# Mamba scan states in SBUF instead of PSUM, decays two steps ahead, four product buffers, mean square on GpSimd

## The chip, the cores and the metric

The kernel runs on one core of a Trainium2 chip. The time is the device time of one launch in microseconds, the median of several runs. The engines are TensorE (PE, with its weight loads as PEld), VectorE (DVE), ScalarE (ACT), GpSimd (POOL) and SyncE (SP), which issues most of the DMAs. They run their own instruction streams and meet only through semaphores.

## The reference

Input `x` is 2 x 2048 tokens of 256 numbers, all in fp32. There are three layers:

```python
x = x + 0.5 * ffn(layernorm(x))     # 8 experts, top 2, capacity 640 a choice
x = x + attn(layernorm(x))          # the Mamba block and a small MLP
x = x + 0.5 * ffn(layernorm(x))
```

The change is in the middle one, where

```python
def attn(x):
    x = x + mamba(rmsnorm(x))
    h = square(relu(rmsnorm(x) @ c_fc_w.T))
    return x + h @ c_proj_w.T

# in mamba: x_conv, z, dt, B and C are projections; 512 channels, 16 states
A = -exp(A_log)
def step(h, inp):
    dt_t, B_t, C_t, u_t = inp
    dA = exp(dt_t[..., None] * A)
    h = h * dA + (dt_t * u_t)[..., None] * B_t[:, None, :]
    y = einsum('bes,bs->be', h, C_t)
    return (h, y)
y = (ys + x_conv * D) * silu(z)
return y @ out_proj_w.T
```

## The kernel before, in words

The program has five parts in a row: routing, experts, `mamba` (the middle layer), routing, experts. Only `mamba` is touched.

`mamba` works in 8 chunks ("turns", index `k`) of 512 tokens. Channels lie on the 128 partitions, in 4 groups `e`, and a turn takes the groups in 2 pairs `p`. For each pair it goes through the 16 states `s`: 32 steps a turn, numbered `n = 16 p + s`, 256 steps in all. One step does, for the two groups of the pair (index `j`):

- ACT: the decay `exp(dt * A)` into a PSUM bank (function `decay`; line 1084 is the helper that records every ACT instruction).
- POOL: `dB = DTU * B` for both groups in one instruction of 1024 elements (line 1260), from the product `DTU` and a row `B` that SP has broadcast into `BC`.
- DVE: the scan over the 512 tokens (line 1363) for each group, `h = h * decay + dB`; a product with `C`, "weigh", for each group into `G` (line 1372); between these two, a copy of the last column of both states into `ST`, masked to zero where a batch ends (line 1379).
- PE: adds each `G` into the output's PSUM bank with an identity matrix (line 1076), two matmuls a step.

The PSUM has 8 banks. Banks 0 and 1 serve all projections in turn, 2 and 3 hold the decays (`B_DA`), 4 and 5 the scan's states (`B_H`), 6 and 7 the output (`B_Y`). So there is one step's worth of decays, and ACT computes those of step `n + 1` after the scans of step `n`. `dB` and `G` have two buffers each.

After a pair's 16 steps `gated` (line 1332) multiplies the two output banks by `silu(z)` into `T3`; before it, line 1327 waits for all of the pair's products on PE. For pair 0 this stands at step 16 behind the scans, for pair 1 at step 0 of the next turn.

The rest of a chunk's work is spread over the steps of the turns around it, by three tables that give for each item the step at which PE, ACT, DVE and POOL do it. `EARLY` is the front of the next chunk: norm, transposes, input projection (`x`, `z`), convolution (`c`, four matmuls with diagonal matrices each, PE items 9, 10, 13 and 14), silu (ACT item 19, with a load of the activation table before and after it), `dt` and its softplus. `LATE` is what is left of it, in the chunk's own turn. `BACK` is the rest of the previous chunk: output projection, RMS norm, MLP. On POOL the items are `add` and `du` (lines 1235 and 1239, 1024 elements each, at steps 27, 28, 6 and 7), `xa` (line 1249, 512 elements, at steps 12 and 14) and the power -1/2 for the RMS norm (line 1245, step 10). On DVE they are `out`, `pj` and `v` (line 1344), which turns ACT's sum of squares `ssq`, 4 numbers a partition, into mean plus eps, at step 8.

An engine does its step's main work first and then the items of that step, DVE its scans first; PE does its items before the step's two products.

## Time and profile before

| | |
|---|---|
| median of 3 runs | 2199.52 us (2195.18 to 2201.32) |
| the profiled execution, its own time | 2204.47 us |
| its span, first to last instruction | 2202.7 us |
| mean granted TensorE clock | 0.941 of full speed |
| busy share of the span | PE 84%, DVE 78%, POOL 56%, ACT 44% |
| first dB product of the stage | 593.4 us |
| last scan of the stage | 1628.1 us |

A share is of the whole span, an average over five parts with different limits. What the change can move lies between the last two rows of the table. Matmul times are modelled in part, and consecutive DVE instructions overlap in the records by some 0.08 us: the next is issued while the last one drains. So the distance from start to start is what a busy DVE pays for an instruction, and the duration is a little more.

### The profile page before, as it was taken

Reading aid. Unit: us, or ns where it says so; the run is one execution under the profiler, and the core shown is the slowest. Engines: PE = TensorE matmul, PEld = TensorE weight load, DVE = VectorE, ACT = ScalarE, POOL = GpSimd, SP = SyncE. Lnnn points to the kernel's source line nnn. Section 1 sums busy time; section 2 is a strip of 40 time slices with the busy share of each in tenths; the row PEclk is TensorE's granted clock in tenths of the full one; section 3 lists DMA queues with packets and bytes.
Section 4 is the critical chain, followed back from the end, with each engine's and each line's share of the span. In section 5 each row is a group of like instructions: output and inputs, shape, how many; then the busy total and the mean of one; then the engine's idle time right before and its main releaser. Section 6 shows DMA issues by size and latency. Waiting matters only on the chain. (4 is left out here: it accounts for less than half of the span.)

```text
span 2202.7 us, 32882 instructions
## 1 busy us (share of the span) xinstructions
PE 1847.9 (84%) x9384; PEld 1306.7 (59%) x9385; DVE 1709.4 (78%) x2990; ACT 968.6 (44%) x1475; POOL 1241.5 (56%) x751
## 2 busy tenths in 40 slices
PE   6379998993887899989999898998577469999996
PEld 6269998993332435434344444434245369999996
DVE  4757667665498989989898999989965667667665
ACT  1333333331455556566655557655441333332331
POOL 1246555555465757667576676757631236555555
PEclk9999999997899999999999999999996579999998
DMA  6244343333333434434343434334412334343442
GB/s 197 72 112 100 80 84 82 81 70 100 115 129 124 134 124 135 133 129 132 125 136 118 133 124 135 134 125 134 143 53 77 115 97 97 80 86 82 85 75 27
DMA packets 160991, 237.52 MB, mean 108 GB/s; under 512 B 29370, under 2 KB 85296, under 8 KB 160304
## 3 DMA queue, kind: packets, MB, share of 16 engines
q1 hardware_dynamic: 130096, 198.84, 28.4%
q0 software_dynamic: 30720, 36.53, 10.0%
q8 instruction: 88, 1.44, 0.3%
q14 instruction: 87, 0.71, 0.1%
HBM read 202.57 MB, written 38.34 MB: 109 GB/s over the span
## 5 line engine op out<-in xcount | busy, mean ns | idle before, releaser
L1260 POOL TENSOR_TENSOR m_dB<-m_DTU,m_BC 128x1024 f32<-128x1024 f32 x256 | 602.8, 2358 | 328.3 <-DVE PS L1363 327.7
L1363 DVE TENSOR_TENSOR_SCAN PS<-PS,m_ST,m_dB 128x512 f32<-128x512 f32 x512 | 629.5, 1276 | 58.3 <-POOL m_dB L1260 27.1
L1076 PE MATMUL PS<-m_G,keep_ident 128*128 128x512 f32 x1024 | 499.4, 612 | 81.6 <-DVE m_G L1372 81.5
L1084 ACT ACTIVATE PS<-m_DT,m_A 128x512 f32<-128x512 f32 x512 | 353.4, 693 | 393.2 <-DVE PS L1363 390.8
L1076 PEld LDWEIGHTS PS<-m_G,keep_ident 128*128 128x128 f32 x1024 | 186.2, 191 | 342.4 <-DVE m_G L1372 211.7
L1372 DVE TENSOR_TENSOR m_G<-PS,m_BC 128x512 f32<-128x512 f32 x512 | 342.1, 679 | 2.9 <-PE PS L1076 2.9
L603 PE MATMUL PS<-e_xh,e_wh 128*128 128x256 f32 x1008 | 293.5, 291 | 0.3 <-DVEq L491 0.2
L603 PE MATMUL PS<-e_xl,e_wh 128*128 128x256 f32 x1008 | 287.4, 285 | 0.0
L603 PE MATMUL PS<-e_xh,e_wl 128*128 128x256 f32 x1008 | 286.9, 285 | 0.0
L621 PE MATMUL PS<-e_wh,e_hh 128*128 128x256 f32 x1008 | 281.6, 279 | 0.0
L660 ACT ACTIVATE e_hh<-e_u 128x512 fp32r<-128x512 f32 x252 | 158.3, 635 | 278.4 <-DVE e_u L716 262.3
L621 PE MATMUL PS<-e_wl,e_hh 128*128 128x256 f32 x1008 | 280.7, 278 | 0.0
L621 PE MATMUL PS<-e_wh,e_hl 128*128 128x256 f32 x1008 | 280.2, 278 | 0.0
L528 POOL DMA_INDIRECT e_xin<-xrows,e_gix x160 | 199.6, 1248 | 57.5 <-issue 45.6
L534 POOL DMA_INDIRECT out<-e_ysb,e_six x80 | 134.5, 1681 | 153.5 <-DVE e_ysb L740 136.5
L534 POOL DMA_INDIRECT sums<-e_ysb,e_six x80 | 135.6, 1696 | 151.3 <-DVE e_ysb L740 134.1
L735 DVE TENSOR_TENSOR e_ysb<-PS,e_b 128x512 f32<-128x512 f32 x80 | 55.2, 691 | 188.7 <-PE PS L621 185.0
L603 PEld LDWEIGHTS PS<-e_xh,e_wh 128*128 128x128 f32 x1008 | 197.1, 196 | 1.0 <-DVEq L491 0.6
L603 PEld LDWEIGHTS PS<-e_xl,e_wh 128*128 128x128 f32 x1008 | 197.1, 196 | 0.0
L603 PEld LDWEIGHTS PS<-e_xh,e_wl 128*128 128x128 f32 x1008 | 195.8, 194 | 0.0
L716 DVE TENSOR_TENSOR e_u<-PS,keep_b 128x512 f32<-128x512 f32 x252 | 170.1, 688 | 25.6 <-PE PS L603 14.1
L621 PEld LDWEIGHTS PS<-e_wl,e_hh 128*128 128x128 f32 x1008 | 189.3, 188 | 0.0
(195 smaller groups left out, 2797.0 us busy)
## 6 DMA issues: line engine op xcount, KB each, us to landing
m_BC<-bc_rows SPq DMA_DIRECT2D x512, 256.0 KB, 3.3
layer_raw<-w SPq DMA_DIRECT2D x64, 512.0 KB
xrows<-r_xn SPq DMA_DIRECT2D x16, 512.0 KB, 4.3
keep_X<-x SPq DMA_DIRECT2D x4, 1024.0 KB, 9.4
sums<-keep_X SPq DMA_DIRECT2D x4, 1024.0 KB, 11.2
out<-keep_X SPq DMA_DIRECT2D x4, 1024.0 KB, 11.1
keep_X<-sums SPq DMA_DIRECT2D x3, 1024.0 KB, 13.3
e_xin<-xrows,e_gix POOLq DMA_INDIRECT x160
```

Of the source, the lines that this page charges most:

```text
L528: G.indirect_dma_start(out=xin[:, c % CPE, t, :], out_offset=None, in_=xrows, in_offset=column(gix, c, t), bounds_check=last_token, oob_is ...
L534: G.indirect_dma_start(out=sums, out_offset=column(six, c, t), in_=ysb[:, c % CPE, t, :], in_offset=None, compute_op=ALU.add, bounds_check ...
L603: last = M(PS[:, B_S1 + pair, m * CH:(m + 1) * CH], a, r, start=(n == 0), stop=(n == len(terms) - 1))
L621: last = M(PS[:, B_Y + c % 2, t * D:(t + 1) * D], a, r, start=(n == 0), stop=(n == len(terms) - 1))
L660: A(hh[:, c % 2, 2 * pair:2 * pair + 2, :], u[:, pair, :, :], ACT.Relu).then_inc(hh_ok, 1)
L716: V.tensor_tensor(u[:, pair, :, :], PS[:, B_S1 + pair, :].rearrange("p (m c) -> p m c", m=2), b1.unsqueeze(2).to_broadcast([P, 2, CH]), AL ...
L735: V.tensor_tensor(ysb[:, c % CPE, :, :], PS[:, B_Y + c % 2, :].rearrange("p (t d) -> p t d", t=CHT), b2.unsqueeze(1).to_broadcast([P, CHT, ...
L1076: last = M(PS[:, B_Y + j, :], C["ident"][:, :], G[:, s % 2, j, :], start=False, stop=(s == DS - 1))
L1084: return nc.scalar.activation(out, in_, func, **kw)
L1260: G_.tensor_tensor(dB[:, s % 2, :, :], DTU[:, es, :], BC[:, s % NBC, 0:1, :].to_broadcast([P, 2, CT]), ALU.mult).then_inc(dB_ok, 1)
L1363: V.tensor_tensor_scan(PS[:, B_H + j, :], PS[:, B_DA + j, :], dB[:, s % 2, j, :], ST[:, s, e:e + 1], ALU.mult, ALU.add).then_inc(scanned, 1)
L1372: V.tensor_tensor(G[:, s % 2, j, :], PS[:, B_H + j, :], BC[:, s % NBC, 1, :], ALU.mult).then_inc(g_ok, 1)
```

## The change

- The scan's output goes to a new SBUF buffer `HS` (two of a pair's size) instead of PSUM banks 4 and 5. The weighing product and the state copy read it there.
- The freed banks hold decays: four banks, two steps' worth. ACT computes the decays of step `n + 2` after the scans of step `n` (`AHEAD = 2`).
- `G` gets four buffers (`NG`) instead of two.
- `v` leaves DVE. ACT's squares are scaled by 1/16 before squaring, so the sum is already the mean; POOL adds eps from a small tile and takes the power, at step 9.
- `T3` and `HID` share one tile `TH` of six groups instead of two tiles of four; the gate product of pair 1 also waits for the last MLP projection of the chunk before.

```diff
+        eps = sb("eps", [P, CTT])
-        T3 = sb("T3", [P, EK, CT])
-        HID = sb("HID", [P, EK, CT])
+        TH = sb("TH", [P, 6, CT])
+        T3 = TH[:, 0:EK, :]
+        def hid(e, n=1):
+            at = e + 4 if e < 2 else e
+            return TH[:, at:at + n, :]
-        G = sb("G", [P, 2, 2, CT])
+        NG, NH = 4, 2
+        G = sb("G", [P, NG, 2, CT])
+        HS = sb("HS", [P, NH, 2, CT])
-        B_DA, B_H, B_Y = 2, 4, 6
+        B_DA, B_Y, AHEAD = 2, 6, 2
-            ..., ("v", 0): (_, _, 8, 10),
+            ..., ("v", 0): (_, _, _, 9),
...
# ACT
-                        last = F(XR[:, t, :], XP[:, t, :], ACT.Square, accum_out=ssq[:, t:t + 1])
+                        last = F(XR[:, t, :], XP[:, t, :], ACT.Square, scale=1.0 / math.isqrt(D), accum_out=ssq[:, t:t + 1])
-                    if not (is_first(k) and n == 0):
-                        act.wait_ge(scanned, k * (2 * STEPS) + (2 * (n - 1) + j + 1))
-                    F(PS[:, B_DA + j, :], DT[:, e, :], ACT.Exp, scale=A[:, e, s:s + 1]).then_inc(dA_ok, 1)
+                    if not (is_first(k) and n < AHEAD):
+                        act.wait_ge(scanned, k * (2 * STEPS) + (2 * (n - AHEAD) + j + 1))
+                    F(PS[:, B_DA + 2 * (n % AHEAD) + j, :], DT[:, e, :], ACT.Exp, scale=A[:, e, s:s + 1]).then_inc(dA_ok, 1)
...
# POOL
                 if kind == "v":
+                    gp.wait_ge(sq_ok, k + 1)
+                    G_.tensor_tensor(ssq[:, :], ssq[:, :], eps[:, :], ALU.add).then_inc(v_ok, 1)
                     gp.wait_ge(v_ok, k + 1)
                     G_.tensor_tensor(ssq[:, :], ssq[:, :], mhalf[:, 0, 0:CTT], ALU.pow).then_inc(rs_ok, 1)
...
# DVE
+                if p == 1 and not (is_first(k)):
+                    wait_written(dve, ("pj", 1), k - 1)
                 V.tensor_tensor(T3[:, es, :], PS[:, B_Y:B_Y + 2, :], SZ[:, par, es, :], ALU.mult).then_inc(yz_ok, 1)
-                elif kind == "v":
-                    dve.wait_ge(sq_ok, k + 1)
-                    V.tensor_scalar(ssq[:, :], ssq[:, :], 1.0 / D, RMS_EPS, ALU.mult, ALU.add).then_inc(v_ok, 1)
-                            if not (is_first(k) and n == 0):
-                                dve.wait_ge(g_ok, k * (2 * STEPS) + (2 * n + j - 1))
-                                dve.wait_ge(kept, k * STEPS + n)
+                            if not (is_first(k) and n < NH):
+                                dve.wait_ge(g_ok, k * (2 * STEPS) + (2 * (n - NH) + j + 1))
+                                dve.wait_ge(kept, k * STEPS + (n - NH + 1))
-                            V.tensor_tensor_scan(PS[:, B_H + j, :], PS[:, B_DA + j, :], dB[:, s % 2, j, :], ST[:, s, e:e + 1],
+                            V.tensor_tensor_scan(HS[:, n % NH, j, :], PS[:, B_DA + 2 * (n % AHEAD) + j, :], dB[:, s % 2, j, :], ST[:, s, e:e + 1],
                                                  ALU.mult, ALU.add).then_inc(scanned, 1)
-                            V.tensor_tensor(G[:, s % 2, j, :], PS[:, B_H + j, :], BC[:, s % NBC, 1, :], ALU.mult).then_inc(g_ok, 1)
+                            V.tensor_tensor(G[:, n % NG, j, :], HS[:, n % NH, j, :], BC[:, s % NBC, 1, :], ALU.mult).then_inc(g_ok, 1)
-                        if not (is_first(k) and n < 2):
-                            dve.wait_ge(g_read, k * STEPS + (n - 1))
+                        if not (is_first(k) and n < NG):
+                            dve.wait_ge(g_read, k * STEPS + (n - NG + 1))
-                        V.tensor_tensor(ST[:, s, 2 * p:2 * p + 2].bitcast(U32), PS[:, B_H:B_H + 2, CT - 1].bitcast(U32),
+                        V.tensor_tensor(ST[:, s, 2 * p:2 * p + 2].bitcast(U32), HS[:, n % NH, :, CT - 1].bitcast(U32),
                                         mask[:, bass.ds(k + 1, 1)].to_broadcast([P, 2]), ALU.bitwise_and).then_inc(kept, 1)
```

## Rows read from the trace of the kernel before

**Rows 1.** Stretches of 128 us from 721 to 1489 us: sum and mean

```profile
sum 768.00, PE 710.38 PEld 329.96 DVE 718.04 ACT 470.77 POOL 515.33; mean PE 118.40 PEld 54.99 DVE 119.67 ACT 78.46 POOL 85.89
```

**Rows 2.** Timeline, one step: start us, us, engine line op

```profile
906.79 2.45 DVE L1363 TENSOR_TENSOR_SCAN PS<-PS,m_ST,m_dB 128x512 f32<-128x512 f32 x2
...
909.15 0.67 DVE L1372 TENSOR_TENSOR m_G<-PS,m_BC 128x512 f32<-128x512 f32 x1
...
909.32 2.35 POOL L1260 TENSOR_TENSOR m_dB<-m_DTU,m_BC 128x1024 f32<-128x1024 f32 x1
...
910.40 2.45 DVE L1363 TENSOR_TENSOR_SCAN PS<-PS,m_ST,m_dB 128x512 f32<-128x512 f32 x2
```

**Rows 3.** Waits of DVE in the stage: us in total, times, longest

```profile
DVE PS L1363 <- ACT PS L1084: 26.6, 8, 3.7
DVE m_T L1332 <- issue: 20.8, 6, 3.5
```

**Rows 4.** Timeline of DVE, two idle times: [idle before <-releaser]

```profile
794.49 1.22 DVE L1332 TENSOR_TENSOR m_T<-PS,m_SZ 128x1024 f32<-128x1024 f32 x1 [3.47 <-issue]
...
815.04 2.47 DVE L1363 TENSOR_TENSOR_SCAN PS<-PS,m_ST,m_dB 128x512 f32<-128x512 f32 x2 [3.47 <-ACT PS L1084]
```

**Rows 5.** Timeline of DVE, routing: sixteen scans of 32 elements

```profile
73.43 2.10 DVE L261 TENSOR_TENSOR_SCAN r_inc<-r_zcol,r_tot 128x32 f32<-128x32 f32 x16
```

**Rows 6.** Groups by line and form, DVE and POOL: busy, mean ns | idle

```profile
L1363 DVE TENSOR_TENSOR_SCAN PS<-PS,m_ST,m_dB 128x512 f32<-128x512 f32 x512 | 629.5, 1276 | 58.3 <-POOL m_dB L1260 27.1 <-ACT PS L1084 26.6 <-issue 3.8
L1372 DVE TENSOR_TENSOR m_G<-PS,m_BC 128x512 f32<-128x512 f32 x512 | 342.1, 679 | 2.9 <-PE PS L1076 2.9
...
L1332 DVE TENSOR_TENSOR m_T<-PS,m_SZ 128x1024 f32<-128x1024 f32 x16 | 19.5, 1216 | 27.3 <-issue 20.8 <-PE PS L1076 6.5
...
L261 DVE TENSOR_TENSOR_SCAN r_inc<-r_zcol,r_tot 128x32 f32<-128x32 f32 x32 | 4.2, 209 | 0.1
...
L264 DVE SCALAR_TENSOR_TENSOR r_pos<-r_pos,r_tot 128x512 f32<-128x512 f32 x2 | 1.4, 692 | 0.1
...
L1260 POOL TENSOR_TENSOR m_dB<-m_DTU,m_BC 128x1024 f32<-128x1024 f32 x256 | 602.8, 2358 | 328.3 <-DVE PS L1363 327.7
...
L1235 POOL TENSOR_TENSOR m_DT<-m_DT,m_sp 128x1024 f32<-128x1024 f32 x16 | 37.7, 2356 | 21.4 <-ACT m_sp L1084 21.4
...
L1249 POOL TENSOR_TENSOR keep_X<-keep_X,m_XP 128x512 f32 x12 | 15.2, 1269 | 0.0
```

**Rows 7.** Timeline of DVE and POOL, expert stage, 404 to 410 us

```profile
404.98 1.28 POOL L516 COPY e_gix<-layer_token 128x10 uint32 x1
...
405.55 0.68 DVE L721 SCALAR_TENSOR_TENSOR e_hl<-e_u,e_hh 128x512 fp32r<-128x512 f32 x1
...
409.76 0.20 POOL L516 COPY e_six<-layer_dest 128x10 uint32 x1
```

**Rows 8.** Line 1344: duration ns, min/median/max, first and last start

```profile
L1344 DVE TENSOR_SCALAR m_ssq<-m_ssq x8: 170/1308/1368, 762.0 to 1645.0; 128x4 f32<-128x4 f32 x8
```

**Rows 9.** Timeline around one of them, POOL and DVE

```profile
760.95 2.36 POOL L1260 TENSOR_TENSOR m_dB<-m_DTU,m_BC 128x1024 f32<-128x1024 f32 x1 [0.65 <-DVE PS L1363]
...
762.03 1.31 DVE L1344 TENSOR_SCALAR m_ssq<-m_ssq 128x4 f32<-128x4 f32 x1
```

**Rows 10.** Timelines of DVE and POOL, routing stage, 83 to 97 us

```profile
83.41 5.46 POOL L341 TENSOR_TENSOR r_hot<-r_count,r_high 128x320 f32<-128x320 f32 x8 [45.76 <-DVEq L288]
...
83.44 5.48 DVE L298 TENSOR_SCALAR r_inlow<-r_count_b,r_low 128x128 bf16<-128x128 bf16 x8 [0.46 <-DVE r_high L287]
...
90.95 0.88 DVE L302 TENSOR_TENSOR r_inblock<-r_hot,r_tile_no 128x320 bf16<-128x320 f32 x2
...
91.22 1.19 POOL L341 TENSOR_TENSOR r_hot<-r_count,r_high 128x320 f32<-128x320 f32 x1 [2.34 <-PE PS L409]
...
91.75 1.39 DVE L298 TENSOR_SCALAR r_inlow<-r_count_b,r_low 128x128 bf16<-128x128 bf16 x2
...
95.81 1.38 DVE L298 TENSOR_SCALAR r_inlow<-r_count_b,r_low 128x128 bf16<-128x128 bf16 x8
```

More of the change, by code:

```diff
@@ L1 @@
+import math
 import concourse.bass as bass
@@ L845, in mamba @@
         BACK = {
-            ("out", 0): (1, _, 2, _), ("out", 1): (3, _, 4, _), ("sq", 0): (_, 7, _, _), ("v", 0): (_, _, 8, 10),
+            ("out", 0): (1, _, 2, _), ("out", 1): (3, _, 4, _), ("sq", 0): (_, 7, _, _), ("v", 0): (_, _, _, 9),
             ("hr", 0): (_, 11, _, _), ("hT", 0): (19, 20, _, _), ("hT", 1): (21, 22, _, _), ("xa", 0): (_, _, _, 12), ("xa", 1): (_, _, _, 14),
@@ L1043, in back @@
                 if kind in ("out", "pj"):
-                    at, ready, src = (W_OUT, yz_ok, T3) if kind == "out" else (W_PJ, q_ok, HID)
+                    at, ready, src = (W_OUT, yz_ok, lambda e: T3[:, e:e + 1, :]) if kind == "out" else (W_PJ, q_ok, hid)
                     pe.wait_ge(ready, k * 2 + 2)
@@ L1048, in back @@
                         for e in range(EK):
-                            last = M(bank(p, k)[:, (t % 2) * D:(t % 2 + 1) * D], src[:, e, t * P:(t + 1) * P],
+                            last = M(bank(p, k)[:, (t % 2) * D:(t % 2 + 1) * D], src(e)[:, 0, t * P:(t + 1) * P],
                                      weights(at, D, e, 0, D), start=(e == 0), stop=(e == EK - 1))
@@ L1075, in turn @@
                             pe.wait_ge(g_ok, k * (2 * STEPS) + (2 * n + j + 1))
-                            last = M(PS[:, B_Y + j, :], C["ident"][:, :], G[:, s % 2, j, :], start=False, stop=(s == DS - 1))
+                            last = M(PS[:, B_Y + j, :], C["ident"][:, :], G[:, n % NG, j, :], start=False, stop=(s == DS - 1))
                         last.then_inc(g_read, 1)
@@ L1177, in back @@
                     wait_written(act, p, k)
-                    F(HID[:, n, :], bank(p, k), ACT.Relu).then_inc(read(p, k), 1)
+                    F(hid(n)[:, 0, :], bank(p, k), ACT.Relu).then_inc(read(p, k), 1)
                 elif kind == "q":
                     wait_read(act, k, ("fc", 2 * n), ("fc", 2 * n + 1))
-                    F(HID[:, 2 * n:2 * n + 2, :], HID[:, 2 * n:2 * n + 2, :], ACT.Square).then_inc(q_ok, 1)
+                    F(hid(2 * n, 2), hid(2 * n, 2), ACT.Square).then_inc(q_ok, 1)
             def decay(k, p, s):
@@ L1191, in decay @@
                     e, n = 2 * p + j, p * DS + s
-                    if not (is_first(k) and n == 0):
-                        act.wait_ge(scanned, k * (2 * STEPS) + (2 * (n - 1) + j + 1))
-                    F(PS[:, B_DA + j, :], DT[:, e, :], ACT.Exp, scale=A[:, e, s:s + 1]).then_inc(dA_ok, 1)
+                    if not (is_first(k) and n < AHEAD):
+                        act.wait_ge(scanned, k * (2 * STEPS) + (2 * (n - AHEAD) + j + 1))
+                    F(PS[:, B_DA + 2 * (n % AHEAD) + j, :], DT[:, e, :], ACT.Exp, scale=A[:, e, s:s + 1]).then_inc(dA_ok, 1)
             def turn(k, par, has_front, has_back):
                 if is_first(k):
-                    decay(k, 0, 0)
+                    for s in range(AHEAD):
+                        decay(k, 0, s)
                 for p in range(PAIRS):
@@ L1201, in turn @@
                         n = p * DS + s
[L1202 to L1203 removed]
+                        if n + AHEAD < STEPS:
+                            decay(k, (n + AHEAD) // DS, (n + AHEAD) % DS)
                         elif has_front:
[L1205 removed]
+                            decay(k + 1, 0, n + AHEAD - STEPS)
                         if is_first(k) and n == FIRST_SILU_AT:
@@ L1270, in _ @@
             V.memset(mhalf[:, :, :], -0.5)
+            V.memset(eps[:, :], RMS_EPS)
             V.memset(fmask[:, :], 1.0)
```

3 lines of the change are left out of this document (removed).

## The prediction

> **What bounds the kernel now.** I read the page first: TensorE (PE) and VectorE (DVE) are the busy engines, and the state-space stage, between the two expert stages, is the only part that the change touches. The view by stretches, cut in pieces of 128 us, about a chunk of 512 tokens each, gives a mean of 119.7 us busy for DVE, 118.4 for PE, 85.9 for GpSimd (POOL) and 78.5 for ScalarE (ACT) [rows 1]. So DVE sets the pace and PE is right behind.
>
> The timeline of one step shows what the DVE time is made of [rows 2]. Two scans are issued at 906.79 and the first product at 909.15, so a scan takes 1.18 us from issue to issue; the product, the small state copy and the second product take 1.25 us (909.15 to 910.40). A step is 3.61 us, without a gap. POOL's dB product, 2.36 us, starts at 909.32, just after the scans end, because it waits for the buffer that they read. It runs beside the two weighing products and is over before the next pair of scans is.
>
> The waits of DVE [rows 3] have two sources that come in every turn: a scan that waits for ACT (26.6 us in 8 waits), and the gate product of line 1332, which waits for PE (20.8 us in 6 waits put down to "issue"; line 1327 asks for every product of the pair). One of each is seen at its place [rows 4]: 3.47 us at 794.49, 3.47 us at 815.04.
>
> **What each part changes.**
>
> *States to SBUF, scan side.* A scan of 32 elements from SBUF to SBUF is issued every 131 ns (16 in 2.10 us) [rows 5]; the one of 512 every 1180 [rows 2]. How much of that is the element and how much a fixed part, neither row tells alone. Products of 512 and 1024 elements take 679 and 1216 ns, 1.05 ns an element; a scan's element needs about twice that, for the two scans, 209 and 1276 ns, lie 2.2 ns an element apart [rows 6]. At exactly twice, 2.10 ns, the 480 further elements cost 1008 ns, and a scan of 512 into SBUF would be issued every 1139 ns, 41 less than now; the recorded durations, treated the same way, give 209 + 1008 = 1217 against 1276, 59 less. Either would be the price of writing PSUM. At 2.19 ns an element there is no such price, and no row shows a slower write to SBUF: bounds 0 and 60 ns. I take 45, near the value from the issue times, which are what a busy engine pays: 512 x 0.045 = 23 us, bounds 0 and 31. In seven of a turn's 32 steps it is lost again, because PE sets the pace between its convolution items (9 to 14) and the gate wait at step 16: 18 us remain.
>
> *States to SBUF, product side.* The product now reads HS and BC, both in SBUF; so does the state copy (HS and the mask). A product of PSUM with SBUF takes 679 ns, a two-input one of the same size with both in SBUF 692 [rows 6]: nothing gained by itself, at most 0.02 us lost. The Trainium skill ("VectorE: DVE Perf Modes", the errata section) has a fixed cost of 58 cycles from SBUF and 120 from PSUM, which would save 65 ns on each of 512 products, 33 us, and put the forecast at 2180. The two rows of this kernel show no such saving, and I use the rows.
>
> *Two SBUF inputs beside POOL.* This is the cost that the diff doesn't name. In the expert stage POOL copies 10 numbers in 0.20 us when DVE is elsewhere, but one that starts at 404.98 takes 1.28 and ends at 406.26, and a DVE instruction with two SBUF inputs (e_u, e_hh) runs from 405.55 to 406.23 [rows 7]: the copy ends 0.03 us after it. The other way round, the 4-element tensor_scalar of line 1344 takes 170 ns once and 1308 in the median [rows 8]; at 762.03 it lasts 1.31 and ends at 763.34, where the dB product begun at 760.95 ends at 763.31 [rows 9]. In the routing stage eight tensor_scalars take 5.48 us beside eight POOL products of 5.46, and 1.38 us without them [rows 10]. So the two engines exclude each other for the length of the reading. The Trainium skill ("SBUF — State Buffer", "Who interferes with whom") says it as a rule: an instruction of VectorE with two SBUF inputs and one of GpSimd that reads SBUF take the same read port in turn, the later blocks fully. The rows agree with it.
>
> By these rows the 512 products and 256 copies, 1.25 us a step, will exclude POOL's 2.36 us, which they now overlap.
>
> What that costs depends on who gets in when. A POOL product waiting behind two DVE products issued back to back (90.95, 0.88 for two) took 1.19 us, to 92.41, where eight unhindered take 0.68 each [rows 10]: counted back from its end it began about when the next DVE instruction was issued (91.75), so its delay covers both and it did not slip in between. If this holds, dB(n+2) waits until the second product is done and runs during the next scans. From a first product at time 0: product, copy, product to 1.25; dB then needs its 2.36, less the tail after its last read (0.14: line 1344 without a wait would have begun at 763.34 - 0.17 = 763.17, and dB ended at 763.31) and less a start-up of a few hundredths that it has behind it, so the port is free at about 3.45. The next product is due at 1.25 + 2 x 1.135 = 3.52 (3.61 if the scan gains nothing). It just fits: no cost a step, and up to 0.1 if a handover is slower, 26 us over 256 steps.
>
> There is no room left in a step, so every other POOL product delays DVE. Those of lines 1235 and 1239, 30 within the stage, have dB's shape and its 2.36 us [rows 6]; their reading holds the port 2.2: 30 x 2.2 = 66 us. Bounds: 33, if half of them fall beside DVE's one-input work, and 66. Those of line 1249 (1.27 us, 14 within the stage, 1.12 each, 15.7 us) stand at items 12 and 14, in front of the gate wait of 3.47 where DVE waits for PE anyhow: nothing, bound 15.7.
>
> *Decays two steps ahead.* ACT does a turn's silu, with a table load before and after it, and the decays stand behind that. With one more step done the scan has 3.5 us more in hand, and the wait was 3.47: the 26.6 us go. Bounds 20 and 26.6.
>
> *Four product buffers.* DVE hardly waits for them; the gate wait is PE's own backlog, which more buffers don't work off. Nothing.
>
> *Mean square on POOL.* Line 1344 goes from DVE: 7 x 1.2 = 8.4 us gained (a wait of 1.31 less the 0.1 that a short instruction takes from issue to issue [rows 9]). POOL gets a 4-element add of some 0.2 us between dB products, and now waits itself for ACT's squares, with its next dB product queued behind; dB is needed a step and a half later, so that hides. T3 and HID sharing a tile adds a wait of the gate product for PE's last projection, which was issued two steps before it and is included in the wait for all products: nothing.
>
> **Sum.** 66 - 18 - 26.6 - 8.4 = +13 us. The sum is made in the profiled execution, 2204.5 us, so 2217.5 there; it stands 5 us above the median of the runs, 2199.5, from which the forecast is 2212.5. Bounds of this case: 33 - 31 x 25/32 - 26.6 - 8.4 = -26 (2173); and 66 + 26 + 15.7 - 0 - 20 - 8.4 = +79 (2279).
>
> **The rivals.**
> *POOL slips in between the products.* If POOL's waiting dB gets the port when the first product is done, the copy and the second product wait out 2.2 us in each of 256 steps: 563 us, with the rest 2199.5 + 563 + 13 = 2,775. For it: eight tensor_scalars and eight POOL products take turns, so a DVE instruction does not keep the port for the next of its kind [rows 10]. Against it: the pair of two-input products at 90.95; but of the 0.27 us from 90.95 to POOL's start only some 0.17 were left to the first one's end, and here POOL will have waited about 0.5.
> *No exclusion that matters* (the other side, faster). If two-input products go beside POOL's reading, or POOL's reading leaves gaps, what remains is -18 - 26.6 - 8.4 = -53, 2146. It decides where POOL's 30 extra products cost under 1.5 us each in place of 2.2 (30 x 1.5 = 45, sum under -6.6). For it: no row shows a two-input tensor_tensor of DVE held up by POOL, only tensor_scalars. Against it: the copy that waits in [rows 7]. PE would allow it: 118.4 busy in 128 us becomes 97% of a turn 5% shorter.
> *The port is shared, but the scan gains nothing*: +31, 2230. *The products gain 65 ns each by leaving PSUM*: 13 - 33, 2180; [rows 6] speak against it, 0.02. Both lie in the first case's range and are counted with it.
>
> **How the numbers follow.** Port in turn, with DVE keeping it through a step: 0.60. POOL slips in: 0.20. No exclusion that matters: 0.20. The first gives 2212.5; its own range is 2173 to 2279, a fifth of it below 2193, a fifth within 0.3% of the median (6.6 us, about what a measurement of this kernel can tell), three fifths above 2206. So faster 0.12 + 0.20 = 0.32, same 0.12, slower 0.36 + 0.20 = 0.56. The range takes in the first and third case, with 8 us below 2146 for the upper bound of the scan's gain, 2138 to 2280, and leaves out the second.
>
> **What the profile of the changed kernel would show.** The scan near 1230 ns in place of 1276. The step from scan to scan at about 3.5 us in quiet stretches, dB products that start just behind the scans but last about 3.5 us in place of 2.36, products of 0.69 us that a few times a turn last near 2.9, next to lines 1235, 1239 and 1249. The wait for ACT near 815 gone, the gate wait still there but shorter. It is wrong if the state copy or second product lasts over 2 us in every step (POOL slips in), if dB stays at 2.36 beside products of 0.69 (no exclusion), or if the scan keeps 1276.

## The result: 21% slower, and all of it in one wait per step

| | before | after |
|---|---|---|
| median of 4 runs, us | 2199.64 (2195.18 to 2201.32) | 2661.97 (2660.71 to 2663.10) |
| ratio, 95% interval | 1 | 1.2106, 1.2085 to 1.2126 |
| the profiled execution: time, span | 2204.47, 2202.7 | 2660.71, 2658.6 |
| stage: start of the first scan to start of the last | 595.9 to 1628.1: 1032.2 | 591.8 to 2084.4: 1492.7 |
| a full turn, first scan to first scan | 129 to 131 | 187.8 (the first 185.2) |

The stage is 460 us longer; the medians differ by 462, the profiled spans by 456. What stands ahead of the stage and behind it took what it took before, within 5 us.

**The groups of the stage**, by line and form (DVE, then POOL), which answer to [rows 6]. L1394 is the state copy, L1387 the product, L1378 the scan, L1274 the dB product:

```profile
L1378 DVE TENSOR_TENSOR_SCAN m_HS<-PS,m_ST,m_dB 128x512 f32<-128x512 f32 x512 | 626.0, 1261 | 25.9 <-POOL m_dB L1274 25.9
L1394 DVE TENSOR_TENSOR m_ST<-m_HS,m_mask 128x2 uint32<-128x2 uint32 x256 | 552.6, 2159 | 0.0
L1387 DVE TENSOR_TENSOR m_G<-m_HS,m_BC 128x512 f32<-128x512 f32 x512 | 361.5, 706 | 0.0
...
L1350 DVE TENSOR_TENSOR m_TH<-PS,m_SZ 128x1024 f32<-128x1024 f32 x16 | 19.1, 1194 | 1.1 <-issue 1.1
```

```profile
L1274 POOL TENSOR_TENSOR m_dB<-m_DTU,m_BC 128x1024 f32<-128x1024 f32 x256 | 683.4, 2670 | 684.2 <-DVE m_HS L1378 684.1
L1251 POOL TENSOR_TENSOR m_DTU<-m_DT,m_U 128x1024 f32<-128x1024 f32 x16 | 45.3, 2833 | 0.1
L1247 POOL TENSOR_TENSOR m_DT<-m_DT,m_sp 128x1024 f32<-128x1024 f32 x16 | 43.8, 2739 | 15.7 <-ACT m_sp L1095 14.7
```

The copy moves two numbers a partition and takes 2159 ns in the mean. The same copy of before stood in this row:

```profile
L1379 DVE TENSOR_TENSOR m_ST<-PS,m_mask 128x2 uint32<-128x2 uint32 x256 | 38.0, 148 | 0.0
```

**One step on the timeline**, DVE and then POOL, which answers to [rows 2]:

```profile
1208.45 0.66 DVE L1387 TENSOR_TENSOR m_G<-m_HS,m_BC 128x512 f32<-128x512 f32 x1
1209.03 2.30 DVE L1394 TENSOR_TENSOR m_ST<-m_HS,m_mask 128x2 uint32<-128x2 uint32 x1
1211.26 0.68 DVE L1387 TENSOR_TENSOR m_G<-m_HS,m_BC 128x512 f32<-128x512 f32 x1
1211.86 2.44 DVE L1378 TENSOR_TENSOR_SCAN m_HS<-PS,m_ST,m_dB 128x512 f32<-128x512 f32 x2
1214.23 0.66 DVE L1387 TENSOR_TENSOR m_G<-m_HS,m_BC 128x512 f32<-128x512 f32 x1
```

```profile
1208.61 2.71 POOL L1274 TENSOR_TENSOR m_dB<-m_DTU,m_BC 128x1024 f32<-128x1024 f32 x1 [3.07 <-DVE m_HS L1378]
```

Read the two together. DVE's first product starts at 1208.45 and ends at 1209.11. dB starts at 1208.61 and lasts 2.71 where it lasted 2.36, which is what it would last if its reading waited for that product's end. The copy is issued at 1209.03 and ends at 1211.33, when dB ends (1211.32). Then the second product runs undisturbed. The step is 5.78 us from product to product, against 3.61. Both engines read two SBUF operands, and here they take turns instruction by instruction. That is the rival "POOL slips in between the products", to which the prediction gave 0.20.

The trap in this view is that no wait shows. DVE has no idle time ahead of the copy; the wait is inside its duration, and DVE's busy share even rises (78% to 84%). An instruction of known size with a duration far over its own is the sign.

**The ledger of the stage**, in us: copies 552.6 - 38.0 = +515; products 361.5 - 342.1 = +19; waits ahead of the scans, 58.3 down to 25.9, -32; gate product, wait 27.3 down to 1.1, -26; line 1344 gone, -9; scans -3.5. Sum +463, measured +460. Busy time is the union of the instructions, so overlaps count once. The two first terms are 239 copies of over 2 us (the other 17 took 0.15) and 15 products of 1.93 to 2.01. Those 15 are the first product of every 16th step, where the gate product stands between the scans and the products: there dB has started 0.9 to 1.0 us ahead, so that the product waits and not the copy. PE was granted 0.84 of its clock from 600 to 2087 us and its products on line 1087 took 753 ns; DVE never waited for them but for the 1.1.

### The profile page after: what moved, and what is told of

The parts are those of the page before. It is cut to its first block and busy times, and to the rows that moved or that the text cites. A ratio compares the mean times of both kernels' runs of the same rounds, so it can differ in the third digit from the quotient of the medians.

```text
span 2658.6 us, 32902 instructions
## 1 busy us (share of the span) xinstructions
PE 2077.9 (78%) x9384; PEld 1332.2 (50%) x9385; DVE 2233.3 (84%) x2983; ACT 968.0 (36%) x1475; POOL 1349.6 (51%) x759
## 5 line engine op out<-in xcount | busy, mean ns | idle before, releaser
L1274 POOL TENSOR_TENSOR m_dB<-m_DTU,m_BC 128x1024 f32<-128x1024 f32 x256 | 683.4, 2670 | 684.2 <-DVE m_HS L1378 684.1
L1087 PE MATMUL PS<-m_G,keep_ident 128*128 128x512 f32 x1024 | 673.0, 753 | 336.1 <-DVE m_G L1387 330.8
L1378 DVE TENSOR_TENSOR_SCAN m_HS<-PS,m_ST,m_dB 128x512 f32<-128x512 f32 x512 | 626.0, 1261 | 25.9 <-POOL m_dB L1274 25.9
L1394 DVE TENSOR_TENSOR m_ST<-m_HS,m_mask 128x2 uint32<-128x2 uint32 x256 | 552.6, 2159 | 0.0
L1387 DVE TENSOR_TENSOR m_G<-m_HS,m_BC 128x512 f32<-128x512 f32 x512 | 361.5, 706 | 0.0
```

The lines of the kernel that those rows point to most:

```text
L1087: last = M(PS[:, B_Y + j, :], C["ident"][:, :], G[:, n % NG, j, :], start=False, stop=(s == DS - 1))
L1274: G_.tensor_tensor(dB[:, s % 2, :, :], DTU[:, es, :], BC[:, s % NBC, 0:1, :].to_broadcast([P, 2, CT]), ALU.mult).then_inc(dB_ok, 1)
L1378: V.tensor_tensor_scan(HS[:, n % NH, j, :], PS[:, B_DA + 2 * (n % AHEAD) + j, :], dB[:, s % 2, j, :], ST[:, s, e:e + 1], ALU.mult, ALU.add ...
L1387: V.tensor_tensor(G[:, n % NG, j, :], HS[:, n % NH, j, :], BC[:, s % NBC, 1, :], ALU.mult).then_inc(g_ok, 1)
L1394: V.tensor_tensor(ST[:, s, 2 * p:2 * p + 2].bitcast(U32), HS[:, n % NH, :, CT - 1].bitcast(U32), mask[:, bass.ds(k + 1, 1)].to_broadcast([ ...
```

## The experiments

Runs of one group shared a chip and the runs of the kernel before. A ratio is to before, with its 95% interval. A kernel without one ran once, and its last column gives the one time of before beside it, in us.

| run | us | ratio, or before beside it |
|---|---|---|
| dB waits for the products | 2261.1 | 1.0275 (1.0249 to 1.0301) |
| state copy on ScalarE | 2645.1 | 1.2017 (1.1986 to 1.2048) |
| PSUM states, the small parts only | 2198.5 | 0.9991 (0.9976 to 1.0006) |
| one SBUF input | 2194.5 | 0.9971 (0.9949 to 0.9993) |
| scans in place | 2219.9 | 1.0083 (1.0062 to 1.0104) |
| in place, decays early | 2182.5 | 0.9909 (0.9875 to 0.9942) |
| the same, z ahead of c | 2169.4 | 0.9855 (0.9823 to 0.9887) |
| z ahead of c, small parts only | 2181.2 | 0.9912 (0.9879 to 0.9944) |
| first product 208, 320 columns | 2582.3, 2611.9 | 2206.3 |
| no wait between, one signal | 2740.0, 2739.3 | 2199.6 |
| equal pair, wait in routing | 2645.2, 2196.2 | 2200.7 |
| bf16 products, third routing product | 2644.7, 2209.3 | 2193.0 |
| repeated factor, plain ones between | 2644.1, 2224.6 | 2204.2 |

### Is it the port, and when POOL asks for it?

**dB waits for the products.** One line of after, on POOL:

```diff
-                            gp.wait_ge(scanned, k * (2 * STEPS) + (2 * n - 2))
+                            gp.wait_ge(g_ok, k * (2 * STEPS) + (2 * n - 2))
```

> The changed kernel, with one wait altered: POOL's dB product waits for the two weighing products of the step (g_ok), not for its scans. If the whole loss comes from the read port being handed to a waiting dB product in front of the state copy, the copy is back at 0.15 us, the second product at 0.69, dB at 2.36 beside the scans, and the step falls from 5.78 to about 3.65 us (1.25 + 2.39); POOL's other large products then have no free port time of their own and cost up to 2.2 us each: 2190 to 2260, 2225 in the middle. If the copy is slow for a reason of its own (a read behind the scan's write to SBUF), it stays at 2.2 to 2.3 us and the kernel near 2660.

Measured: 2261.1, so 401 of the 462 us come back by moving one start. Timeline of DVE and of POOL, a crowded step and the start of a quiet one at 908.24:

```profile
906.18 1.47 DVE L1387 TENSOR_TENSOR m_G<-m_HS,m_BC 128x512 f32<-128x512 f32 x1
907.57 0.15 DVE L1394 TENSOR_TENSOR m_ST<-m_HS,m_mask 128x2 uint32<-128x2 uint32 x1
907.64 0.68 DVE L1387 TENSOR_TENSOR m_G<-m_HS,m_BC 128x512 f32<-128x512 f32 x1
908.24 2.45 DVE L1378 TENSOR_TENSOR_SCAN m_HS<-PS,m_ST,m_dB 128x512 f32<-128x512 f32 x2
```

```profile
904.74 2.35 POOL L1274 TENSOR_TENSOR m_dB<-m_DTU,m_BC 128x1024 f32<-128x1024 f32 x1
908.40 2.35 POOL L1274 TENSOR_TENSOR m_dB<-m_DTU,m_BC 128x1024 f32<-128x1024 f32 x1 [1.30 <-DVE m_G L1387]
```

dB now runs beside the scans, one of whose inputs is PSUM, and has its 2.35 back; the copy is 0.15 again. The product at 906.18 waits because that dB came late, behind the two POOL instructions of the mean square (902.6 to 904.8). This kernel is the schedule that the prediction described as its likeliest case, made by a semaphore, so it prices that case's terms. Of its 255 steps 162 are under 3.8 us: 117 take 3.62 to 3.66 and 45 take 3.71 to 3.74, where a quiet step of before takes 3.62. So the handover costs 0.04 in most steps and 0.10 in some, 0.05 in the mean and about 8 us in all. The extra POOL work: 37 copies over 0.3 us carry 64.5 us above 0.15 each, 15 products over 0.83 carry 17.6 above 0.68. By what POOL runs beside them, lines 1247 and 1251 cost 29.4 + 32.2 = 61.6 us (the prediction has 66), line 1263 15.0 (0, bound 15.7), and the mean square 7 x 0.79 = 5.5, which the prediction took to hide.

**The state copy on ScalarE.** After, with DVE's copy between the products taken out:

```diff
# ACT, after step n's decays
+                        act.wait_ge(scanned, k * (2 * STEPS) + (2 * n + 2))
+                        F(ST[:, s, 2 * p:2 * p + 2], HS[:, n % NH, :, CT - 1], ACT.Copy, scale=now[:, 0:1]).then_inc(kept, 1)
```

> The changed kernel with the state copy made by ACT, so that the two weighing products stand back to back on DVE with dB waiting behind the first. Theory 1 (a waiting POOL product gets the port at the first change of instruction after it asked, whatever follows): the second product lasts about 2.8 us in every step, the step stays near 5.7 us, 2630 to 2660. Theory 2 (DVE keeps the port from one product to the next of its kind, and only the state copy gave it away): the second product lasts 0.68, dB lasts about 3.5 from its start, the step is 3.6, 2190 to 2240.

Measured: 2645.1. Two products now follow each other on DVE, and the second takes the blow: 0.66, then 2.83, under a dB of 2.71 (the first line holds both, 3.42 from start to end).

```profile
902.86 3.42 DVE L1395 TENSOR_TENSOR m_G<-m_HS,m_BC 128x512 f32<-128x512 f32 x2
906.21 2.45 DVE L1386 TENSOR_TENSOR_SCAN m_HS<-PS,m_ST,m_dB 128x512 f32<-128x512 f32 x2
```

So the copy was no special victim: whatever comes second waits, and like instructions do not keep the port between them here.

**A first product of 208 and of 320 columns**, which shortens the time between POOL's start and DVE's next instruction (it leaves out the rest of the first product).

```diff
-                            V.tensor_tensor(G[:, n % NG, j, :], HS[:, n % NH, j, :], BC[:, s % NBC, 1, :], ALU.mult).then_inc(g_ok, 1)
+                            V.tensor_tensor(G[:, n % NG, j, 0:(208 if j == 0 else CT)], HS[:, n % NH, j, 0:(208 if j == 0 else CT)], BC[:, s % NBC, 1, 0:(208 if j == 0 else CT)], ALU.mult).then_inc(g_ok, 1)
```

> The changed kernel with the first product cut to 208 of its 512 columns (the rest of that product is left out and stays zero), so that DVE issues the state copy about 0.28 us after it and dB, which starts 0.155 us after the first product, has waited about 0.13 us at that moment, as the POOL product of the routing stage in [rows 10] had. If a POOL instruction asks for the port some time after its recorded start, longer than 0.13 us, the copy goes through in 0.15 us and the second product, issued 0.07 us later, waits instead (2.8 us). If it asks at once, the copy waits 2.3 us. If DVE keeps the port where instructions follow close, neither waits: a step of 3.3 us and under 2150.

> The same with 320 columns (the other 192 left out): the copy is issued about 0.40 us after the first product, and dB has waited about 0.24 us. If POOL asks within 0.24 us, the copy waits 2.3 us in every step, as with 512 columns; if later, the copy goes through and the second product waits 2.8 us.

```profile
1205.11 0.34 DVE L1388 TENSOR_TENSOR m_G<-m_HS,m_BC 128x208 f32<-128x208 f32 x1
1205.38 2.30 DVE L1395 TENSOR_TENSOR m_ST<-m_HS,m_mask 128x2 uint32<-128x2 uint32 x1
```

```profile
1205.27 2.39 POOL L1274 TENSOR_TENSOR m_dB<-m_DTU,m_BC 128x1024 f32<-128x1024 f32 x1 [3.07 <-DVE m_HS L1379]
```

The copy is issued 0.11 us after dB's start and still waits 2.30; with 320 columns the gap is 0.23 and the wait the same. An engine that has been waiting a tenth of a microsecond is served first.

**One SBUF input.** After, with the products' factor and the copy's mask read from PSUM banks that hold constants, and the decays one step ahead again to free those banks (it leaves out C's change from step to step and the reset between batches):

```diff
-                            V.tensor_tensor(G[:, n % NG, j, :], HS[:, n % NH, j, :], BC[:, s % NBC, 1, :], ALU.mult).then_inc(g_ok, 1)
+                            V.tensor_tensor(G[:, n % NG, j, :], HS[:, n % NH, j, :], PS[:, B_C, :], ALU.mult).then_inc(g_ok, 1)
...
-                        V.tensor_tensor(ST[:, s, 2 * p:2 * p + 2].bitcast(U32), HS[:, n % NH, :, CT - 1].bitcast(U32),
-                                        mask[:, bass.ds(k + 1, 1)].to_broadcast([P, 2]), ALU.bitwise_and).then_inc(kept, 1)
+                        V.tensor_tensor(ST[:, s, 2 * p:2 * p + 2], HS[:, n % NH, :, CT - 1],
+                                        PS[:, B_C + 1, 0:2], ALU.mult).then_inc(kept, 1)
```

> The changed kernel with its states in SBUF as they are, but with no DVE instruction of two SBUF inputs: both products read their factor from a PSUM bank that holds one row of C all along (left out: the C of each step), and the state copy is multiplied by ones in PSUM (left out: the reset between the two batches). Two of the four decay banks are taken for that, so the decays are one step ahead, as before. If the read port is the whole loss, the copy is back at 0.15, the products at 0.68, dB at 2.36 from just behind the scans, the step at 3.6, and the time at 2190 to 2205. If SBUF states cost something by themselves (a scan that writes SBUF, a read behind it), the time stays above 2215; if the scan gained 45 ns each, it falls below 2185.

```profile
L1383 DVE TENSOR_TENSOR_SCAN m_HS<-PS,m_ST,m_dB 128x512 f32<-128x512 f32 x512 | 628.3, 1270 | 36.6 <-ACT PS L1095 28.5 <-issue 4.1 <-POOL m_dB L1274 3.2
L1392 DVE TENSOR_TENSOR m_G<-m_HS,PS 128x512 f32<-128x512 f32 x512 | 340.3, 674 | 0.0
L1399 DVE TENSOR_TENSOR m_ST<-m_HS,PS 128x2 f32<-128x2 f32 x256 | 38.8, 152 | 0.0
```

2194.5, with dB at 2359 ns beside the products. The second SBUF operand is the whole loss. The states in SBUF cost nothing and give nothing that these runs can tell: the scan takes 1270 ns, the product 674 with one PSUM input, and the ratio (0.9949 to 0.9993) overlaps that of the next kernel, whose states are in PSUM (0.9976 to 1.0006). The Trainium skill ("SBUF — State Buffer", "Who interferes with whom") says that an instruction of VectorE with at most one SBUF input, outside its 2-port modes, does not contend with GpSimd, and that one with two SBUF inputs contends with a GpSimd instruction that reads SBUF. This run and after agree with both halves.

### What the other parts are worth

**PSUM states, the small parts only**: before, with the mean square on POOL, four product buffers and the shared tile, and nothing else.

```diff
-        G = sb("G", [P, 2, 2, CT])
+        G = sb("G", [P, 4, 2, CT])
...
-            ..., ("v", 0): (_, _, 8, 10),
+            ..., ("v", 0): (_, _, _, 9),
```

> The kernel before with three parts of the change: mean square finished by POOL, four product buffers, T3 and HID in one tile. The states stay in PSUM, the decays one step ahead. By the sum only the first counts: 7 x 1.2 us, so 8 us faster than before, 2191; the buffers nothing. A rival gives the buffers part of the gate wait (20.8 us): down to 2175.

2198.5: no difference that shows. Timeline of DVE at the two idle times of [rows 4]:

```profile
795.54 1.22 DVE L1346 TENSOR_TENSOR m_TH<-PS,m_SZ 128x1024 f32<-128x1024 f32 x1 [4.68 <-issue]
...
816.08 2.47 DVE L1374 TENSOR_TENSOR_SCAN PS<-PS,m_ST,m_dB 128x512 f32<-128x512 f32 x2 [3.59 <-ACT PS L1092]
```

The 1.2 us that DVE saved on line 1344 came back as 1.2 us more in front of the gate product (3.47 to 4.68), where PE sets the time. The interval of the ratio, 5 us faster to 1 us slower, leaves the term of 8.4 us out.

**Scans in place**, to get the decays ahead without SBUF states: the kernel above, with each scan written over its own decays in PSUM.

```diff
# the scan's output and first input
-                            PS[:, B_H + j, :], PS[:, B_DA + j, :]
+                            PS[:, B_DA + 2 * (n % 2) + j, :], PS[:, B_DA + 2 * (n % 2) + j, :]
# ACT, ahead of the decays of step n
-                        act.wait_ge(scanned, k * (2 * STEPS) + (2 * (n - 1) + j + 1))
+                        act.wait_ge(g_ok, k * (2 * STEPS) + (2 * (n - 2) + 2))
+                        act.wait_ge(kept, k * STEPS + (n - 2 + 1))
```

> As the kernel e3_psum_states, and each scan writes its states over its own decays in PSUM, so that four banks give decays two steps ahead without any SBUF state: the decays of step n + 2 wait for the products of step n. If the port is all that made the change slow, the wait for ACT (26.6 us) goes too: 2199.6 - 8 - 26 = 2165, products at 0.68, copy at 0.15, dB at 2.36. If PE's backlog at the gate product takes up what is gained, 2180 to 2191. If a scan in place is slower, its record shows it above 1276 ns.

> As e4_inplace, but the decays of step n + 1 wait for the products of step n - 1 and are issued in ACT's step n, so ACT's items come earlier than in the kernel before and not later, as they did in e4_inplace (2220). If the later items made e4_inplace slow, the wait for ACT falls from 3.5 to about 1 us a turn, the gate wait stays near 4.7: 2199 - 8 x 2.5 = 2180. If a turn's length is set by PE alone, what the ACT wait loses comes back at the gate, and the time stays within 5 us of 2199.

The first form, which issues the decays of step n + 2 after step n, is slower (2219.9). They now wait for the products, and ACT's items of each step stand behind them. The wait for ACT falls from 27.0 to 13.7 us, but the gate wait grows to 5.55 a turn, and the scans' wait for dB from 28.5 to 51.3 in all, because POOL's two long items of a turn start late and run back to back with dB (752 to 764 us). The second issues the decays of n + 1 ahead of step n's items, as before; it waits only for products long done. 2182.5: the wait for ACT falls from 27.0 us (longest 3.7) to 17.4 (2.2), all idle time ahead of the scans from 60.0 to 43.4, and the gate wait stays at 4.7. The scan takes 1276 ns in place as well.

**z ahead of c**: the front's z projections move to PE's steps 13 to 16 and the last two convolutions behind them, to 17 and 18, out of the way of the pair's last product. Once on the kernel above, once on the one with the small parts only.

```diff
-            ..., ("c", 2): (13, 14, _, _),
-            ("c", 3): (14, 15, _, _), ("z", 0): (15, 16, _, _), ("z", 1): (16, 17, _, _), ("z", 2): (17, 18, _, _),
-            ("z", 3): (18, 19, _, _), ...
+            ..., ("z", 0): (13, 14, _, _),
+            ("z", 1): (14, 15, _, _), ("z", 2): (15, 16, _, _), ("z", 3): (16, 17, _, _), ("c", 2): (17, 18, _, _),
+            ("c", 3): (18, 19, _, _), ...
```

> As e7_inplace_early, with PE's z projections moved from steps 15 to 18 to steps 13 to 16, and two of the four convolutions from 13 and 14 to 17 and 18. A convolution item costs PE 3.4 us on top of 1.7 for the products, 1.5 more than a DVE step; that backlog is what the gate product at step 16 waits for. If so, the gate wait of 3.5 to 4.7 us falls to about 1.5 and the time to 2180 - 25 = 2155; if the backlog only moves to the silu behind the convolutions, the wait for ACT grows by as much and the time stays at 2180.

> As e3_psum_states (2198.5), with the same swap of z and convolution items and nothing else. If the gate wait is PE's backlog of four convolutions, it falls by 3 us in each of 8 turns: 2175. If silu, now behind the last convolution at step 18, comes later by what the backlog is, the wait for ACT at step 20 grows from 3.5 to 6 us: 2198.

Groups of DVE in the combined kernel:

```profile
L1372 DVE TENSOR_TENSOR_SCAN PS<-PS,m_ST,m_dB 128x512 f32<-128x512 f32 x512 | 629.9, 1277 | 59.9 <-ACT PS L1092 35.7 <-POOL m_dB L1271 24.2
...
L1347 DVE TENSOR_TENSOR m_TH<-PS,m_SZ 128x1024 f32<-128x1024 f32 x16 | 19.5, 1216 | 12.0 <-issue 9.0 <-PE PS L1084 3.1
```

The gate wait falls from 36 us to 12 here and 13 in the other; part of it comes back as a wait for ACT, 17.4 to 35.7 us here and 27.0 to 34.2 in the other. Combined, 2169.4, the best here: 1.5% under before, with the states still in PSUM.

### Why did the pair in [rows 10] stay together?

The prediction had read its schedule from that pair. Eight more runs vary the pair, from the kernel with the copy on ScalarE or from before.

**No wait between, and no signal either**: both scans are waited for ahead of the first product; in the second run one signal covers both products.

```diff
-                            dve.wait_ge(scanned, k * (2 * STEPS) + (2 * n + j + 1))
+                            if j == 0:
+                                dve.wait_ge(scanned, k * (2 * STEPS) + (2 * n + 2))
```

> As e2_copy_on_act (2645: two products back to back, the second waits 2.2 us for dB), but both scans are waited for ahead of the first product, so the second has no wait of its own, as the second of the pair at 90.95 in the routing stage [rows 10] had none. If a wait in front of an instruction is what opens the port for POOL, the second product lasts 0.68, the step is 3.6 and the kernel about 2230. If not, the step stays at 5.7 and the time at 2645.

> As e12_no_wait_between, and the first product signals no semaphore (the second counts for both), so the pair is joined as the pair of the routing stage was: no wait and no signal between. If the signal at its end is what opens the port, 2230; if neither, 2645, and the routing pair was let through for something in its own shape (three-dimensional operands, 320 elements, bf16 out) or in POOL's.

```profile
1205.96 3.44 DVE L1396 TENSOR_TENSOR m_G<-m_HS,m_BC 128x512 f32<-128x512 f32 x2
```

```profile
1205.90 2.35 POOL L1282 TENSOR_TENSOR m_dB<-m_DTU,m_BC 128x1024 f32<-128x1024 f32 x1 [4.19 <-DVE m_HS L1386]
```

For dB neither answers. With both engines released by the same scan, dB starts 0.05 us ahead of the first product, and that one now waits: the pair was not parted, it was preceded. The step is 5.95 us, the longest of all.

POOL's other instructions answer in the same traces. In the second run 30 of them start during a first product, and all get in ahead of the second one, though nothing stands between the two: 12 of `du` (1024 elements; the second product then lasts 2.82), 12 of `xa` (512 elements; 1.75) and 6 additions of 4 numbers, which are over 0.14 us after the second product's start. DVE and POOL at one `xa`, where the first line holds both products, 2.84 behind dB and 1.75 behind `xa`:

```profile
1046.74 4.51 DVE L1396 TENSOR_TENSOR m_G<-m_HS,m_BC 128x512 f32<-128x512 f32 x2
```

```profile
1048.99 1.72 POOL L1271 TENSOR_TENSOR keep_X<-keep_X,m_XP 128x512 f32 x1
```

**An equal pair.** As the run without wait and signal, but both products read the first group's states, so that the first needs only the first scan (it leaves out the second group's products).

```diff
-                                dve.wait_ge(scanned, k * (2 * STEPS) + (2 * n + 2))
+                                dve.wait_ge(scanned, k * (2 * STEPS) + (2 * n + 1))
-                            last = V.tensor_tensor(G[:, n % NG, j, :], HS[:, n % NH, j, :], BC[:, s % NBC, 1, :], ALU.mult)
+                            last = V.tensor_tensor(G[:, n % NG, j, :], HS[:, n % NH, 0, :], BC[:, s % NBC, 1, :], ALU.mult)
```

> The kernel after with the state copy on ScalarE, the two products without a wait or a signal between them (both signals come with the second), and both of them multiplying the states of the pair's first group, so that the first can start as early as ever, beside the second scan's end (it leaves out the products of the second group, so the output is not the reference's). GpSimd's dB then starts behind the first product, as in the kernel after, and finds a DVE instruction queued with nothing between. Theory 1, what parted the products before was the wait or the signal between them, and two products with nothing between keep the port, as the pair of the routing stage does: the second product 0.66 us, dB about 3.3, step near 3.7, some 2,200 to 2,230 us. Theory 2, GpSimd gets the port at any change of instruction: second product 2.83, dB 2.71, step 5.7, about 2,645 us. In both, the start of dB must be read first: if it starts ahead of the first product, as in the two runs before, the run does not answer.

```profile
1003.36 3.43 DVE L1396 TENSOR_TENSOR m_G<-m_HS,m_BC 128x512 f32<-128x512 f32 x2
```

```profile
1003.51 2.72 POOL L1282 TENSOR_TENSOR m_dB<-m_DTU,m_BC 128x1024 f32<-128x1024 f32 x1 [2.99 <-DVE m_HS L1386]
```

dB starts 0.15 us after the first product, and the second, with nothing between the two, lasts 2.85: parted, 2645.2 us.

**A wait in routing**, the other way round:

```diff
                     for c in range(TOPK):
+                        dve.wait_ge(abs_ok, i * (2 * NH) + (2 * g + 2))
```

> The kernel before, with one more wait, already met, ahead of each of the two products of line 302 in the routing stages; nothing else is changed. Theory 1, a wait between two DVE instructions is what lets GpSimd in: the second product of the pair beside GpSimd's waiting one (90.95 in the trace of before) grows from 0.48 to about 1.1 us, and GpSimd's shrinks from 1.19 to about 0.9. Theory 2, the wait is nothing: 0.48 and 1.19 as before. The time of the whole kernel stays within 0.3% in both.

Still 0.48 each and 1.19 to 1.20 for POOL, in all four places of the two routing stages. Wait and signal have no part in it.

**The type of the output, the form of the factor, the time.** Four edits: `G` and its identity in bf16; the factor four numbers of C, each repeated 128 times; in routing a third product between the two; in routing three products with two plain factors between them.

```diff
-        G = sb("G", [P, NG, 2, CT])
+        G = sb("G", [P, NG, 2, CT], BF16)
...
# the factor of the products, the other two operands viewed as 4 x 128
-                                            BC[:, s % NBC, 1, :]
+                                            BC[:, s % NBC, 1, 0:4].unsqueeze(2).to_broadcast([P, 4, CT // 4])
...
# routing, between the two products of line 302
+                            for r in range(3):
+                                V.tensor_tensor(spare[:, g, r, :, :], hot[:, g, 0, :, :], hot[:, g, 1, :, :], ALU.mult)
```

> The kernel after with the state copy on ScalarE, and the products and their identity matrix on TensorE in bf16, which is what the pair of the routing stage writes. Theory 1, a product that writes 16-bit values is over sooner or keeps the port: second product near 0.66, step under 4 us, about 2,200 us. Theory 2, the type of the output has no part in it: second product 2.83, dB 2.71, step 5.7, about 2,645 us, as with fp32.

> The kernel before, with a third product of the same kind between the two of line 302 in the routing stages, into a tile of its own that nobody reads. GpSimd's instruction starts some 0.27 us after the first of them, so it sees two changes of a two-input instruction in place of one. Theory 1, at its start GpSimd is just too late for the first change and gets in at the next: the first two last 0.48 us, the third about 1.0, and GpSimd 1.19. Theory 2, these products keep the port between them whatever the time: all three last 0.48 and GpSimd about 1.6, until the next tensor_scalar. The whole kernel is longer by 8 to 20 us, 40 products or so at 0.40.

> The kernel after with the state copy on ScalarE, and products whose second factor is a repeated value: four numbers of C, each read for 128 elements, in place of 512 of them (it leaves out the rest of C, so the output is not the reference's). The pair of the routing stage reads its second factor so. Theory 1, an input that repeats one value leaves no two-input reading, or keeps the port: second product near 0.66, dB either 2.36 (no exclusion) or 3.3 (it waits for the pair), step 3.7, about 2,200 us. Theory 2, the factor's form has no part in it: second product 2.83, dB 2.71, step 5.7, about 2,645 us.

> The kernel before, with three products between the two of line 302 in the routing stages, whose two factors are both plain rows of 320 numbers in SBUF, into a tile that nobody reads. Theory 1, the repeated second factor of line 302 is what keeps the port: GpSimd, which starts during the first, gets in at a change of the plain ones, one of them lasts about 1.0 us or more, and GpSimd's instruction about 1.0 to 1.2. Theory 2, it is something of GpSimd's own instruction or of the stage: all five products last 0.48, and GpSimd about 2.4, until the next tensor_scalar. The kernel is longer by some 40 us (120 products at 0.40 is 48, less where the stage has time to spare).

In the Mamba stage the second product lasted 2.82 and 2.83 us. In routing three products stayed together; timeline of DVE and of POOL in the run with the third one:

```profile
97.94 0.48 DVE L303 TENSOR_TENSOR r_inblock<-r_hot,r_tile_no 128x320 bf16<-128x320 f32 x1
98.34 0.48 DVE L306 TENSOR_TENSOR r_spare<-r_hot,r_tile_no 128x320 bf16<-128x320 f32 x1
98.74 0.48 DVE L303 TENSOR_TENSOR r_inblock<-r_hot,r_tile_no 128x320 bf16<-128x320 f32 x1
99.14 1.38 DVE L299 TENSOR_SCALAR r_inlow<-r_count_b,r_low 128x128 bf16<-128x128 bf16 x2
```

```profile
98.19 1.60 POOL L345 TENSOR_TENSOR r_hot<-r_count,r_high 128x320 f32<-128x320 f32 x1 [3.06 <-PE PS L413]
```

POOL waits through two changes of instruction, ends 0.05 us ahead of the first tensor_scalar (99.14, 0.70) and so got the port at the change to it. With three plain products between the two, all five lasted 0.48 and POOL 2.40. Both runs show it in all four places. So the reading of [rows 10] was right: there DVE keeps the port through two, three and five such products. It did not carry over to the Mamba stage. Excluded as the reason, each taken by itself, are a wait, a signal, the output's type, a repeated factor, and being just too late; so is the length of POOL's instruction, as those of 1024, 512 and 4 elements all got in. What remains are the length of the products (320 against 512, though a 320-column product followed by the copy was parted), and the form of POOL's instruction, which in routing subtracts two operands that are both repeated. No run tells these apart, or tests two features at once; the cause stays open.

## Why the prediction was wrong

**The step that failed** is the one in "What that costs depends on who gets in when": that a waiting dB "did not slip in between" and would run behind the second product. In place of it, POOL was served at DVE's first change of instruction, in 239 of 256 steps, at 2.15 us each, and the range of 2138 to 2280 had left that case out. Everything before that step held: two SBUF inputs and POOL's reading exclude each other for their length (one SBUF input: 2194.5). The rival's price, 563 us, came to 515 in the copies, and to 533 with the 15 long products. The other 30 are 0.93 less in each of those 15 steps, the last two steps, which had no dB beside them, and 0.05 less in each of the 239. The rival's whole sum, 2775, was 113 too high: these 30, the 66 for POOL's extra products, which cost nothing here, and 32 for waits of DVE that went beyond the 26.6 of the sum (26 at the gate, 6 ahead of the scans), less 15 for the scans, which gained 3.5 and not 18. The prediction rested the choice on one pair of another stage, with other lengths and another POOL instruction, and noted against itself that "a DVE instruction does not keep the port for the next of its kind" in the alternating tensor_scalars of the same rows. Two rows that disagree about the one fact on which 560 us hang are no ground for 0.60 to 0.20.

**Term by term.** *Scan, -18 us*: 1261 ns against 1276 recorded, but from issue to issue 2.37 us for a pair against 2.36, so nothing; its lower bound, 0, was right. In the estimate a fixed part was carried over from scans of 32 elements, which these runs do not bear out. *Products reading SBUF*: 674 with a PSUM input, 0.66 to 0.68 undisturbed with two from SBUF; no 65 ns, as the rows had said. *The 30 extra POOL products, +66 us*: in after they cost nothing, because they start when the second product has just started, wait 0.5 us for its end and read during the scans (2739 and 2833 ns in place of 2356). In the schedule for which the term was made, the first experiment gives 62, and 15 for line 1263. *Wait for ACT, -26.6*: gone in after, where DVE is late anyhow. In a kernel of the old pace, getting the decays earlier left 17.4 of 27.0 us (scans in place, decays early), because silu and its two table loads keep ACT for 6.3 us there (800.38 to 806.70), against a step of 3.6. *Mean square, -8.4*: about 0, as the gate wait took it up, and with the schedule of the first experiment POOL's part costs 5.5. *Four product buffers, the shared tile*: 0, as said. *Handover*: 0.05 us a quiet step in the first experiment, taken as 0 in the sum, with 0.1 as its bound.

So even with its schedule made true, the sum would have fallen short, by 48 us (2212.5 against 2199.64 x 1.0275 = 2260). The terms found wrong are 15 for line 1249's products (1263 in after), 8 for the handover (0.05 in 162 quiet steps), 18 for the scan and 8 + 5 for the mean square, less 4 for lines 1247 and 1251: 50 together, which is the shortfall within what these runs can tell.

## What to carry to other kernels

Before moving an operand from PSUM to SBUF, list every DVE instruction that then has two SBUF inputs and every POOL instruction that reads beside it; count, as in this stage, one full POOL duration for each meeting, unless a semaphore keeps POOL's instruction behind them. If the freed banks are the aim, look for another source first: here the scan could be written over its own input, and the decays came early with the states still in PSUM. Work taken off an engine just ahead of a wait for another engine comes back as more of that wait, so look for the next wait before counting a saving.

## What the runs showed of the hardware

- A wait for the shared port is inside the duration: 2 numbers a partition took 2.30 us, with no idle time shown on DVE.
- In the Mamba stage POOL is served at DVE's next instruction: dB after only 0.11 us of waiting, instructions of 512 and 4 elements after 0.51 and 0.29. And a POOL instruction that starts 0.05 us ahead blocks the first of two products outright (2.84 us).
- In the routing stage the same engines with two-input products of 320 elements made POOL wait through two, three and five in a row (1.19, 1.60, 2.40 us), in all four places of each trace. Nothing here explains the difference.
- A scan written over its own PSUM input takes the time of one that is not: 1276 ns.
